# Moving the attention scores into a PSUM bank and giving each of two engines a whole tile to weigh

## The reference

```python
qh = _split_heads(q @ Wq.T)                 # q is the layernorm of x, 16 heads of 32
k_sel, v_sel = kh[b_idx, :, gc], vh[b_idx, :, gc]     # four rows per token, gc = seg_id - 0..3
scores = jnp.einsum('bhqd,bhqkd->bhqk', qh, k_sel) * SCALE
scores = jnp.where(neg_mask[:, None, :, :], neg_inf, scores)
probs = jax.nn.softmax(scores, axis=-1)
out = jnp.einsum('bhqk,bhqkd->bhqd', probs, v_sel)
return out @ Wo.T                           # then x = x + this
```

## Time and profile before

| | value |
|---|---|
| median of three runs | 2336.34 us |
| profiled execution, own time | 2335.28 us |
| its span | 2333.4 us |
| attention, first product to last h_peak | 60.5 to 633.6 us |
| first matmul of the feed forward | 645.94 us |
| VectorE busy over the span | 1766.4 us |
| GpSimd busy over the span | 667.4 us |
| TensorE busy over the span | 2019.0 us |
| ScalarE busy over the span | 1349.1 us |

### The profile page before, as it was taken

How to read it: one execution, slowest core, us unless ns; L and a number is a source line. 1 busy time by engine, 2 the same in 40 slices (tenths; PEclk the granted TensorE clock), 3 DMA queues, 4 the chain that set the end, 5 groups by cost and what they waited for, 6 DMA issues and landing times.

```text
span 2333.4 us, 25335 instructions
## 1 busy us (share of the span) xinstructions
PE 2019.0 (87%) x9524; PEld 944.9 (40%) x9524; DVE 1766.4 (76%) x1404; ACT 1349.1 (58%) x1571; POOL 667.4 (29%) x664
## 2 busy tenths in 40 slices
PE   5888888888599999999999999999100799999998
PEld 2444444444344444444444444444000344444443
DVE  8799999999746756665599999999699744457541
ACT  4678788887422322222399886766699633446430
POOL 2599999999300000000011101222010000000000
PEclk9999999999899999999999999999655899999999
DMA  7789999998346755753699986886899855555641
GB/s 297 278 316 336 353 331 349 338 343 334 126 158 234 243 216 196 250 180 134 236 406 416 413 341 251 292 320 253 355 418 372 317 224 216 208 204 217 234 153 72
DMA packets 132025, 637.74 MB, mean 273 GB/s; under 512 B 12352, under 2 KB 12864, under 8 KB 91968
## 3 DMA queue, kind: packets, MB, share of 16 engines
q1 hardware_dynamic: 86464, 318.91, 37.4%
q0 software_dynamic: 45440, 317.21, 34.8%
HBM read 431.73 MB, written 204.34 MB: 273 GB/s over the span
## 4 chain that ended last, share of the span: by engine, by line
PE 64%; issue 2%; ACT 2%; DVE 2%; DMA 1%; POOL 0%; DVEq 0%; ACTq 0%; POOLq 0%
PE fd_pp L1810 43%; PE fd_pp L1824 21%; ACT ff_ring L1753 1%; DMA ff_ring<-gate_integers 1%; DVE ff_sig L1609 1%; DMA kept_gate<-gate_integers 0%; DVE ff_h_parts L1593 0%; ACT kept_gate L1757 0%; DVE ff_sq L1529 0%; ACT ff_gin L1757 0%; DVE ff_sq L1600 0%; ACT ff_hq L1757 0%; POOL ff_o_all L898 0%; ACT ff_sig L1740 0%; ACT ff_ring L1779 0%
## 5 line engine op out<-in xcount | busy, mean ns | idle before, releaser
L1824 PE MATMUL fd_pp<-ff_down,kept_gate 128*128 128x512 f16 x1536 | 458.3, 380 | 181.4 <-DVE ff_up L1650 181.4
L1810 PE MATMUL fd_pp<-ff_h_parts,kept_gate 128*128 128x512 f16 x2304 | 499.4, 380 | 14.2 <-DVE ff_h_parts L1421 14.2
L1810 PE MATMUL fd_pp<-ff_h_parts,ff_up 128*128 128x512 f16 x2304 | 497.4, 379 | 0.0
L1673 ACT ACTIVATE ff_raw<-fd_pp 128x1024 f32<-128x1024 f32 x192 | 195.1, 1020 | 399.5 <-PE fd_pp L1810 394.4
L1810 PEld LDWEIGHTS fd_pp<-ff_h_parts,kept_gate 128*128 128x128 f16 x2304 | 225.8, 98 | 287.7 <-DVE ff_h_parts L1421 14.6
L1810 PEld LDWEIGHTS fd_pp<-ff_h_parts,ff_up 128*128 128x128 f16 x2304 | 225.4, 98 | 271.9
L1824 PEld LDWEIGHTS fd_pp<-ff_down,kept_gate 128*128 128x128 f16 x1536 | 150.5, 98 | 363.7 <-issue 183.3
L1824 PE MATMUL fd_pp<-ff_down,ff_up 128*128 128x512 f16 x768 | 291.7, 380 | 0.0
L1437 DVE TENSOR_REDUCE ff_gate_top<-ff_raw 128x1 f32<-128x2048 f32 (+1 forms) x49 | 109.8, 2242 | 187.2 <-ACT ff_raw L1673 187.2
L1779 ACT ACTIVATE ff_ring<-ff_hq,kept_g 128x2048 int16<-128x2048 f32 x48 | 96.1, 2001 | 229.0 <-DVE ff_hq L1583 226.3
L790 PE MATMUL at_psO<-kept_wo,at_ahi 128*128 128x512 f16 x512 | 155.6, 386 | 36.2 <-ACT at_alo L277 31.6
(11 more groups left out here) (244 smaller groups left out, 3375.2 us busy)
## 6 DMA issues: line engine op xcount, KB each, us to landing
ff_raw<-up_scratch SPq DMA_DIRECT2D x66, 1024.0 KB, 8.4
gate_scratch<-ff_raw POOLq DMA_DIRECT2D x48, 1024.0 KB, 8.9
ff_gin<-gate_scratch SPq DMA_DIRECT2D x48, 1024.0 KB, 8.8
up_scratch<-ff_raw POOLq DMA_DIRECT2D x48, 1024.0 KB, 8.6
ff_gin<-gate_integers SPq DMA_DIRECT2D x77, 512.0 KB, 6.3
gate_integers<-ff_ring POOLq DMA_DIRECT2D x43, 512.0 KB, 11.5
ff_up<-up_scratch SPq DMA_DIRECT2D x21, 1024.0 KB, 8.8
kept_xs<-in_x SPq DMA_DIRECT2D x32, 512.0 KB, 14.6
```

The costliest lines, as they stand in the source:

```text
L1673: nc.scalar.activation(raw[:, n % UNITS, h * 2 * BLK:(h + 1) * 2 * BLK], pp[(2 * n + h) % 4][:, :, :].rearrange("p a t -> p (a t)"), ACT.C ...
L1810: mm = nc.tensor.matmul(pp[k % 4][:, h, :], wt[w][:, c, f:f + P], a[:, b % 2, :, c, :], start=(q == 0), stop=(q == len(todo) - 1))
L1824: mm = nc.tensor.matmul(pp[k % 8 // 2][:, k % 2, :], a[b % 2][:, f, t * P:(t + 1) * P], wt[w][:, f, :], start=(q == 0 and i == 0), stop=(q ...
```

## The change

The masked scores, the exponentials and the even tile's shares move from SBUF into one PSUM bank, `psS`. The odd tile's shares stay in SBUF, as `odd_pr`. VectorE weighs all four value rows of the even tile in one instruction; GpSimd weighs all four of the odd tile in one. GpSimd no longer waits for VectorE's weighing before it starts. To free a bank, the second `psH` goes: from tile 58 on the bank `psX`, which is out of use by then, takes its place. The layernorm scales on GpSimd take three instructions in place of four (the factor 1/512 goes into the first).

```diff
-        sc, ex, pr = (r.sb(n, [P, 2, W, H], F32) for n in ("sc", "ex", "pr"))
-        raw = ds = sc
+        odd_pr = r.sb("odd_pr", [P, W, H], F32)
...
+        psS = r.ps("psS", [P, 4, 2 * W * H])
+        sc, ex = (psS[:, i, :].rearrange("p (a w h) -> p a w h", a=2, w=W) for i in range(2))
+        even_pr = psS[:, 2, 0:W * H].rearrange("p (w h) -> p w h", w=W)
+        raw = ds = sc
...
-        psH = [r.ps(f"psH{i}", [P, DC, P]) for i in range(2)]
+        psH = r.ps("psH", [P, DC, P])
+        END = LAST - 5
+
+        def h_bank(t):
+            return psX if t >= END and (t - END) % 2 else psH
...
-                def weigh(t):
-                    values = kv[:, t % KR, 0:W - 1, D:2 * D].rearrange("p w (h e) -> p w h e", h=H)
-                    nc.vector.tensor_tensor(values, values, pr[:, t % 2, 0:W - 1].unsqueeze(3).to_broadcast([P, W - 1, H, HD]),
+                def weigh_even(p):
+                    t = 2 * p
+                    values = kv[:, t % KR, :, D:2 * D].rearrange("p w (h e) -> p w h e", h=H)
+                    dve.wait_ge(m["even_pr"], p + 1)
+                    nc.vector.tensor_tensor(values, values, even_pr.unsqueeze(3).to_broadcast([P, W, H, HD]),
                                             ALU.mult).then_inc(m["pv"], 1)
...
-                        need(dve, m["last"], a)
-                        nc.vector.tensor_tensor(pr[:, :, :, :], ex[:, :, :, :], inv[:, :, :].unsqueeze(2).to_broadcast([P, 2, W, H]),
-                                                ALU.mult).then_inc(m["pr"], 1)
-                        dve.wait_ge(m["pr"], s_ + 1)
-                        weigh(a)
+                        nc.vector.tensor_tensor(even_pr, ex[:, 0], inv[:, 0].unsqueeze(1).to_broadcast([P, W, H]),
+                                                ALU.mult).then_inc(m["even_pr"], 1)
+                        need(dve, m["odd_pv"], s_)
+                        nc.vector.tensor_tensor(odd_pr[:, :, :], ex[:, 1], inv[:, 1].unsqueeze(1).to_broadcast([P, W, H]),
+                                                ALU.mult).then_inc(m["odd_pr"], 1)
+                        weigh_even(s_)
                         if s_ == NP - 1:
                             sum_last(a)
                             residual(a - 2)
-                        weigh(a + 1)
-                        if s_ == NP - 1:
+                            weigh_last()
                             sum_last(a + 1)
...
-                    nc.gpsimd.tensor_tensor(sqe[:, k], ssq[:, r, k], eps_d[:, k], ALU.add).then_inc(m["sqe"], 1)
+                    nc.gpsimd.tensor_scalar(sqe[:, k], ssq[:, r, k], 1.0 / D, EPS, ALU.mult, ALU.add).then_inc(m["sqe"], 1)
                     pool.wait_ge(m["sqe"], n)
-                    nc.gpsimd.tensor_tensor(root[:, k], sqe[:, k], expo[:, k], ALU.pow).then_inc(m["root"], 1)
-                    pool.wait_ge(m["root"], n)
...
-                    nc.gpsimd.tensor_tensor(rstd[:, r, k], root[:, k], root_d[:, k], ALU.mult).then_inc(m["rstd"], 1)
+                    nc.gpsimd.tensor_tensor(rstd[:, r, k], sqe[:, k], expo[:, k], ALU.pow).then_inc(m["rstd"], 1)
...
-                def weigh_fourth(t):
-                    last = kv[:, t % KR, W - 1, D:2 * D].rearrange("p (h e) -> p h e", h=H)
+                def weigh_odd(p):
+                    t = 2 * p + 1
+                    w0 = 2 if t == LAST else 0
+                    values = kv[:, t % KR, w0:W, D:2 * D].rearrange("p w (h e) -> p w h e", h=H)
                     pool.wait_ge(rows_in[t % KR], 16 * (t // KR + 1))
-                    pool.wait_ge(m["pr"], t // 2 + 1)
-                    if t < LAST - 1:
-                        pool.wait_ge(m["pv"], t // 2 * 2 + 2)
-                    nc.gpsimd.tensor_tensor(last, last, pr[:, t % 2, W - 1].unsqueeze(2).to_broadcast([P, H, HD]),
-                                            ALU.mult).then_inc(m["last"], 1)
+                    pool.wait_ge(m["odd_pr"], p + 1)
+                    nc.gpsimd.tensor_tensor(values, values, odd_pr[:, w0:W].unsqueeze(3).to_broadcast([P, W - w0, H, HD]),
+                                            ALU.mult).then_inc(m["odd_pv"], 1)
...
                 for s_ in range(NP + 6):
-                    if s_ == NP:
-                        weigh_fourth(LAST - 1)
-                        weigh_fourth(LAST)
+                    if pair(s_ - 1):
+                        weigh_odd(s_ - 1)
...
                 def turn_h(t):
                     pe.wait_ge(m["hn"], t + 1)
-                    need(pe, m["hT_sb"], t - 1)
-                    turn(psH[t % 2], hn[:, t % 2, :]).then_inc(m["hT"], 1)
+                    if t >= END and (t - END) % 2:
+                        pe.wait_ge(m["xlo"], NT)
+                    need(pe, m["hT_sb"], t - 1 if t > END else t)
+                    turn(h_bank(t), hn[:, t % 2, :]).then_inc(m["hT"], 1)
```

More of the change, by code:

```diff
@@ L114, in opening @@
     nmean, ssq, rstd, shift = (keep[n] for n in ("nmean", "ssq", "rstd", "shift"))
-    sqe, root, eps_d, expo, root_d = (keep[n] for n in ("sqe", "root", "eps_d", "expo", "root_d"))
+    sqe, eps_d, expo = (keep[n] for n in ("sqe", "eps_d", "expo"))
     wq, wo, ident = keep["wq"], keep["wo"], keep["ident32"]
@@ L187, in opening @@
         rows_in = [r.sem(f"rows_in{i}") for i in range(KR)]
-        m = r.sems("xn xT xhi xrest xlo q prod raw sc top ds ex tot inv pr pv last half att aT ahi arest alo o x1 "
-                   "nmean ssq ssq_v stat aggr sqe root rstd norm x_nmean x_ssq hn hT hT_sb peak h_red h_all reduced")
+        m = r.sems("xn xT xhi xrest xlo q prod raw sc top ds ex tot inv even_pr odd_pr pv odd_pv half att aT ahi arest alo o x1 "
+                   "nmean ssq ssq_v stat aggr sqe rstd norm x_nmean x_ssq hn hT hT_sb peak h_red h_all reduced")
         def blocks(t, h):
@@ L323, in take_hT @@
                     need(act, hT_out[p % 2], 16 * (p // 2))
-                    nc.scalar.activation(hT[:, t % 4, :], psH[t % 2][:, :, :].rearrange("p c t -> p (c t)"),
+                    nc.scalar.activation(hT[:, t % 4, :], h_bank(t)[:, :, :].rearrange("p c t -> p (c t)"),
                                          ACT.Copy).then_inc(m["hT_sb"], 1)
@@ L391, in _ @@
                         act.wait_ge(m["ds"], s_ + 1)
-                        need(act, m["pr"], s_)
-                        nc.scalar.activation(ex[:, :, :, :], ds[:, :, :, :], ACT.Exp).then_inc(m["ex"], 1)
+                        need(act, m["odd_pr"], s_)
+                        nc.scalar.activation(ex, ds, ACT.Exp).then_inc(m["ex"], 1)
                     if s_ == 1:
@@ L540, in sum_last @@
                 def sum_last(t):
-                    dve.wait_ge(m["last"], t + 1)
-                    dve.wait_ge(m["pv"], t + 1)
+                    dve.wait_ge(m["pv"], NP + t - (LAST - 1))
+                    dve.wait_ge(m["att"], t)
+                    if t == LAST:
+                        dve.wait_ge(m["odd_pv"], NP)
                     nc.vector.tensor_tensor(kv[:, t % KR, 0:2, D:2 * D], kv[:, t % KR, 0:2, D:2 * D], kv[:, t % KR, 2:4, D:2 * D],
@@ L574, in _ @@
                         nc.vector.scalar_tensor_tensor(
-                            out=sc[:, :, :, :].rearrange("p a w h -> p (a w) h"), in0=raw[:, :, :, :].rearrange("p a w h -> p (a w) h"),
+                            out=sc.rearrange("p a w h -> p (a w) h"), in0=raw.rearrange("p a w h -> p (a w) h"),
                             scalar=keep["alpha"][:, 9:10],
@@ L579, in _ @@
                         dve.wait_ge(m["sc"], s_ + 1)
-                        nc.vector.tensor_reduce(top[:, :, :], sc[:, :, :, :].rearrange("p a w h -> p a h w"), AX.X,
+                        nc.vector.tensor_reduce(top[:, :, :], sc.rearrange("p a w h -> p a h w"), AX.X,
                                                 ALU.max).then_inc(m["top"], 1)
@@ L682, in gather @@
                                                 element_offset=0).then_inc(rows_in[t % KR], 16)
-                def weigh_fourth(t):
-                    last = kv[:, t % KR, W - 1, D:2 * D].rearrange("p (h e) -> p h e", h=H)
+                def weigh_odd(p):
+                    t = 2 * p + 1
+                    w0 = 2 if t == LAST else 0
+                    values = kv[:, t % KR, w0:W, D:2 * D].rearrange("p w (h e) -> p w h e", h=H)
                     pool.wait_ge(rows_in[t % KR], 16 * (t // KR + 1))
-                    pool.wait_ge(m["pr"], t // 2 + 1)
-                    if t < LAST - 1:
-                        pool.wait_ge(m["pv"], t // 2 * 2 + 2)
-                    nc.gpsimd.tensor_tensor(last, last, pr[:, t % 2, W - 1].unsqueeze(2).to_broadcast([P, H, HD]),
-                                            ALU.mult).then_inc(m["last"], 1)
+                    pool.wait_ge(m["odd_pr"], p + 1)
+                    nc.gpsimd.tensor_tensor(values, values, odd_pr[:, w0:W].unsqueeze(3).to_broadcast([P, W - w0, H, HD]),
+                                            ALU.mult).then_inc(m["odd_pv"], 1)
                 def add_up(t):
```

(8 more changed lines are left out.)

12 lines of the change are left out of this document (8 added, 4 removed).

## The result

The changed kernel takes 2300.6 us, median of four runs (2298.91 to 2302.64), beside 2336.24 us for the kernel before on the same chip. The ratio is 0.985, 95% interval 0.9838 to 0.9861. The forecast was 2304 us in a range of 2296 to 2320, faster. The profiled execution took 2300.15 us with a span of 2298.4 us, 35.0 us less than the span before.

A forecast was written before the change was run, and what follows sets the result against it. VectorE was taken as the bound, at 16.94 us a slot. Savings of 22.6 (24 full slots at 16.0), 6.6 (six others), 0.9 (early GpSimd meeting) and 1.2 (last slot) total 31.3 us, giving 2304 from 2335.28; range 2296 to 2320.

The forecast's parts named there:

- VectorE's slot, 15.61 plus 0.2 for the bank: VectorE's slot, product to product, falls from 16.94 to 15.61 us; small instructions writing or reading PSUM add 0.2: 15.8.
- The stretch comes from two SBUF inputs: VectorE instructions with both inputs in SBUF hold GpSimd up: its shift takes 1.59 us beside the weighing, 0.19 otherwise.
- GpSimd's iteration 15.56: GpSimd's work per slot after the change sums to 15.56 us, ends 15.3 and 15.9, with the odd weighing at 3.9.
- Rival D: GpSimd's four-row weighing with repeated shares is dearer; over 5.3 us it sets the slot; at 6.1, 2359 us; chance 0.07.
- C: VectorE's weighing with a PSUM input blocks GpSimd just the same; shift stays 1.6 us; no change, 2333 to 2343; chance 0.04.
- The ring at 15.92: ScalarE and TensorE hand over to each other: 5.97, 5.58 and 4.69 us, less a 0.31 wait on VectorE, limit the slot.
- the third piece: Part of the ScalarE and TensorE handovers, from `take_xlo` at 308.53 until ScalarE's work ends at 313.22: 4.69 us.
- Rival A: The shorter slot is held by ScalarE and TensorE's handovers or by DMA at about 16.4 us; 2317 us; chance 0.19.
- B: ScalarE and TensorE's handovers are no limit and PSUM costs VectorE nothing; slot 15.6 us throughout, 2293 us; chance 0.06.
- DMA fits with nothing to spare: At a 16.0 us slot DMA moves 355 GB/s, busy share 0.97 to 1.0; its floor is 15.6 us.
- The other six slots: Slots 2 to 4 and 29 to 31: ScalarE has less to do, VectorE's 15.8 holds, gaining 6 x 1.1 = 6.6 us.
- The tail: In the last slot VectorE no longer idles 0.94 us for GpSimd or has its addition stretched, gaining 1.2 us.

The follow-up runs named there:

- the fastest run: Changed kernel with ScalarE's means of `x` moved to the slot before and VectorE's maximum over the even tile's result alone, a probe: 2278.55 us, ratio 0.9753.

## Why the prediction was right, point by point

**VectorE was the bound, GpSimd only looked full.** Right, and shown from two sides: in the kernel before, shorter norms on GpSimd alone are worth nothing (2334.54 us), and 0.28 us less on VectorE makes the slot 0.28 shorter (16.66). After the change GpSimd is no bound either: a fourth instruction in the norms costs nothing (2300.2 us).

**VectorE's slot, 15.61 plus 0.2 for the bank.** The first part was right: weighing 2.28, mask 0.36. The bank's price, taken at plus 0.2, had the wrong sign. The maximum went from 0.37 to 0.29 and the sum from 0.36 to 0.29, the subtraction from 0.29 to 0.30, the sums of the products from 2273 to 2282 ns. VectorE's own slot is 15.54 beside its wait, 15.45 where it has none, so 15.61 less 0.16. By the Trainium skill's "VectorE: DVE Perf Modes", the errata section, reading PSUM costs 62 cycles more per instruction (120 for 58); the measurement decides against it here, and VectorE's slot of 16.0 by that rule did not come.

**The stretch comes from two SBUF inputs.** Right. With only the even shares in SBUF the whole gain is gone, with everything in SBUF 21 of 36 us are. What was missing is that the loss depends on what is met, and that VectorE's small instructions are held by GpSimd's additions as well.

**GpSimd's iteration 15.56.** Its terms add up to 15.54. It is 15.02 to 15.08. The weighing is 3.64, at the low end of 3.6 to 4.2: the fixed part is that of the additions. Rival D needed over 5.3 and is out; so is C, with the shift at 0.20.

**The ring at 15.92, and 16.0 for a full slot.** The step held: ScalarE's wait for VectorE and the query's wait for the product went, and the ring stayed, 15.83 by the rows. Two small terms were too large. The 0.08 us that I added for three loops close together did not come. And the ring itself is 0.09 shorter than its sum: the third piece, 4.69, was read to the end of ScalarE's last instruction (313.22), but ScalarE starts its next instruction 0.1 us before such an end (at 312.42 behind 312.32 + 0.19 before), and the piece measures 4.59. So 24 slots gave 26.7 us for 22.6, 4.1 more. The tail gave 1.9 more, the other slots 1.1 less, and the stretches outside lost 1.2. Together that is 3.7 us more span than the 31.3 forecast; the time is 3.4 us below 2304. Rival A (held at 16.4) and B (15.6 throughout) are out by the slot itself; the run with the means moved earlier shows that the ring was what B lacked.

**DMA fits with nothing to spare.** It does: at 0.99 busy no product waits for rows, and in the fastest run, at 15.01 us a slot and a share of 1.00, none does either; there only the loads of `x` begin to be late.

**The other six slots.** Expected 6.6 + 0.9, measured 6.4, and that this is near is luck. VectorE's 15.8 does not hold in the early ones: slots 2 and 3 take 16.29 and 16.48, and VectorE waits 2.52 and 2.06 us for the exponential in them. ScalarE has fewer instructions there, but waits longer for TensorE. So the three early slots gave 2.0 us instead of 3.3 and the 0.9 for the early meeting. The late ones gave 4.4 instead of 3.3: two of them take 15.46.

**The tail.** Expected 1.2, measured 3.1. The term that I gave was right: VectorE gave 1.3 (the turn of the last but one `att` starts 6.64 us after the last sum before, 5.30 after). What the sum left at nothing is TensorE's clock behind that turn. The twelve matmuls of the next projection run from 612.49 to 616.71 before and from 578.15 to 580.74 after, 4.22 us for 2.59, and that is 1.6 of the other 1.8:

```profile
612.49 1.06 PE L790 MATMUL at_psO<-kept_wo,at_ahi 128*128 128x512 f16 x2
...
616.71 0.60 PE L797 MATMUL at_psH<-kept_ident,at_hn 128*128 128x128 f32 x4
```

```profile
578.15 0.59 PE L806 MATMUL at_psO<-kept_wo,at_ahi 128*128 128x512 f16 x2
...
580.74 0.60 PE L813 MATMUL at_psH<-kept_ident,at_hn 128*128 128x128 f32 x4
```

The granted clock is 0.61 in this stretch before, so mostly at the 1.2 GHz level, and 1.00 after, the 2.4 GHz level. TensorE had idled 1.87 us ahead of the turn before, and 0.90 after. Why the clock fell in the one case and not in the other is not shown.

## What to carry to other kernels

When two engines look full, look for tiny instructions that are long: they may be held by the other engine, and only one of the two is then the bound. An operand of a long VectorE instruction that moves from SBUF to PSUM can be worth more to GpSimd than to VectorE. And add up the ring of handovers between the remaining engines before the change is made: it tells where the gain ends, and where an instruction can be moved into an idle time to get past it.

## What the runs showed of the hardware that was not expected

- Small VectorE reductions over 128 strided numbers are shorter from PSUM than from SBUF, 0.29 against 0.36 to 0.37 us; element by element instructions are not (0.30 against 0.29 for the subtraction, 0.36 against 0.35 for the mask where it meets nothing).
- Exclusion works by instruction. VectorE's weighing waited 0.59 us for a GpSimd addition to end, and the next addition 1.94 us for the weighing; but a power of four columns that had begun ran on beside it (1.09 us against 1.04), and the weighing took its 2.28 all the same. GpSimd's additions of 512 and 1024 numbers that had begun did hold a VectorE subtraction (0.89 us at 312.57, 1.92 at 196.74, for 0.29).
- ScalarE's exponential over 128 numbers takes 0.25 us from PSUM to PSUM and 0.31 in SBUF.
- GpSimd's multiplication with a share repeated 32 times costs 3.64 us for 2048 numbers, 1.05 for 512; an addition of 1024 costs 2.37.
